# Two softmax attentions with the layers between them issued as jobs by 512 tokens, and inverse roots by Newton steps

## What is computed

```python
h = layernorm(x) * (1 + ca) + sa
y = softmax(mask(rope(h@Wq.T+bq) @ rope(h@Wk.T+bk).T / sqrt(16))) @ (h@Wv.T+bv)   # 16 heads of 16, causal
x = x + ga * (y @ Wo.T + bo)
h = layernorm(x) * (1 + cb) + sb
hidden = h                                   # the second ffn has an attention of its own
a = rmsnorm(hidden, ln1_w)
attn = softmax(mask(heads(a@Wq.T) @ heads(a@Wk.T).T / 4)) @ heads(a@Wv.T) @ Wo.T
mod = 0.1 * tanh(attn @ A)
g = rmsnorm(hidden, ln2_w)
x = x + gb * (hidden + (silu(g@W_in.T + mod*(g@A)@B) * (g@W_up.T)) @ W_down.T)
```

## Time and profile before

| | before |
|---|---|
| time, median of 3 runs (lowest, highest) | 732.89 us (732.44, 736.16) |
| the profiled execution: its own time, its span | 735.81 us, 734.0 us |
| PE busy (share of the span) | 655.8 us (89%) |
| PE weight loads | 415.0 us (57%) |
| DVE, ACT, POOL busy | 473.3 (64%), 347.5 (47%), 169.3 (23%) |
| mean granted TensorE clock | 0.957 |

### The profile page before, as it was taken

The page is one execution under the profiler, slowest core; times in us unless marked ns, Lnnn a source line. Parts: engine busy times, 40 slices in busy tenths (PEclk is TensorE's granted clock), DMA queues, the critical chain, the costliest instruction groups (busy, mean ns, idle before and its releaser), DMA issues.

```text
span 734.0 us, 10645 instructions
## 1 busy us (share of the span) xinstructions
PE 655.8 (89%) x3934; PEld 415.0 (57%) x3939; DVE 473.3 (64%) x955; ACT 347.5 (47%) x558; POOL 169.3 (23%) x209
## 2 busy tenths in 40 slices
PE   4997867999999897699999998787899999999996
PEld 3785635777677676345544434464454444368885
DVE  6777685777677378398888801586589887232323
ACT  4554233443333434325466685462455667843332
POOL 3434214554555235311000000000000001003221
PEclk9999689999999999899999999999799999989998
DMA  8820000002000003733000000026430000050001
GB/s 297 257 71 19 1 21 1 21 23 79 0 1 0 1 1 114 226 93 88 2 2 1 2 2 0 1 82 218 132 89 2 2 2 2 10 165 1 0 1 57
DMA packets 36327, 38.34 MB, mean 52 GB/s; under 512 B 3954, under 2 KB 35200, under 8 KB 36020
## 3 DMA queue, kind: packets, MB, share of 16 engines
q1 hardware_dynamic: 36276, 37.67, 16.3%
HBM read 30.12 MB, written 7.34 MB: 51 GB/s over the span
## 4 chain that ended last, share of the span: by engine, by line
PE 48%; issue 17%; POOL 13%; DVE 11%; ACT 5%; SPq 2%; DMA 2%; POOLq 0%; ACTq 0%; DVEq 0%
PE psum L782 10%; PE psum L768 8%; PE psum L745 8%; POOL it_lo L1700 8%; PE psum L456 3%; PE psum L457 3%; PE psum L458 2%; POOL wd L1675 2%; PE psum L771 2%; SPq L412 2%; PE psum L496 2%; PE psum L748 2%; PE psum L473 2%; POOL t L1650 2%; PE psum L575 1%
## 5 line engine op out<-in xcount | busy, mean ns | idle before, releaser
L966 ACT ACTIVATE pt<-psum 128x1024 f32<-128x1024 f32 (+1 forms) x192 | 148.2, 811 | 94.5 <-PE psum L771 66.1
L1320 DVE TENSOR_REDUCE mx<-psum 128x1 f32<-128x512 f32 (+3 forms) x216 | 132.4, 665 | 16.3 <-PE psum L745 8.3
L745 PE MATMUL psum<-kr,qr 96*128 96x512 bf16 (+3 forms) x384 | 109.9, 336 | 5.2 <-DVE m L1320 1.8
L768 PE MATMUL psum<-qr,kr 99*128 99x512 bf16 (+3 forms) x384 | 99.1, 331 | 5.2 <-DMA qr<-m3T 3.7
L1700 POOL TENSOR_TENSOR it_lo<-it,it_hi 128x512 fp32r<-128x512 f32 x48 | 66.5, 1385 | 153.4 <-ACT it_hi L1017 153.4
L456 PE MATMUL psum<-h_hi,wf_hi 128*128 128x512 f32 x192 | 76.5, 398 | 7.0 <-DVE wf_lo L1381 4.0
L782 PE MATMUL psum<-pt,vp 128*32 128x512 f32 (+3 forms) x768 | 81.7, 498 | 0.0
L1017 ACT CAST it_hi<-it 128x512 fp32r<-128x512 f32 x48 | 29.8, 622 | 97.3 <-DVE it L1393 97.3
L457 PE MATMUL psum<-h_lo,wf_hi 128*128 128x512 f32 x192 | 75.6, 394 | 0.0
L458 PE MATMUL psum<-h_hi,wf_lo 128*128 128x512 f32 x192 | 75.5, 393 | 0.0
L745 PEld LDWEIGHTS psum<-kr,qr 96*128 96x128 bf16 x384 | 36.6, 99 | 68.3 <-DVE mx L1320 29.4
(11 more groups left out here) (209 smaller groups left out, 1132.0 us busy)
## 6 DMA issues: line engine op xcount, KB each, us to landing
parts_scratch<-parts SPq DMA_DIRECT2D x16, 384.0 KB, 3.5
qr<-parts_scratch SPq DMA_DIRECT2D x48, 128.0 KB, 2.6
kr<-parts_scratch SPq DMA_DIRECT2D x48, 128.0 KB, 2.7
wmod<-in_L_wmod SPq DMA_DIRECT2D x1, 1536.0 KB, 6.1
x<-in_L_attn_x SPq DMA_DIRECT2D x2, 512.0 KB, 4.1
wmod<-in_L_wmod SPq DMA_DIRECT2D x1, 1024.0 KB, 7.8
packed<-in_L_ffn_gate_W_packed SPq DMA_DIRECT2D x1, 1024.0 KB, 9.8
packed<-in_L_ffn_up_W_packed SPq DMA_DIRECT2D x1, 1024.0 KB, 11.8
```

What stands on the lines that cost most here:

```text
L745: m = pe.matmul(b, qr[0:PARTS_ROWS, c, h, (qt - 4 * c) * P:(qt - 4 * c + 1) * P], kr[0:PARTS_ROWS, ch, h, 0:w], start=True, stop=not diag)
L768: m = pe.matmul(bank[4 + 2 * at[0] + j][:, 0:w], kr[0:PARTS_ROWS + 3, kt // 4, h, (kt % 4) * P:(kt % 4 + 1) * P], qr[0:PARTS_ROWS + 3, c, ...
L966: act.activation(pt[:, n % 4, :, 0:w], psum[:, b:b + 2, 0:w], ACT.Exp, scale=0.25).then_inc(S["ex"], 1)
L1320: dve.tensor_reduce(dst, bank[at[0]][:, 0:k * w].rearrange("p (k w) -> p k w", k=k), AX, ALU.max).then_inc(S["p1_mx"], 1)
```

## The change

1. `attention_order()` becomes `attention_orders()` and makes one list for each attention. Besides banks, rowmax, scores, values and outs they hold **jobs** (`JOBS`), which are the bridge cut in pieces for 512 tokens. The bridge of tokens 0 to 511 (with the small product `woa` ahead) stands in the list of attention 0, behind `out 3`, when block 3 has finished these tokens. The bridge of tokens 512 to 1023 stands in the list of attention 1, between its blocks of c = 0. A job with a product takes a bank of the ring of three. Banks of c = 1 come in attention 1 only behind the last job of the chain.
2. Both inverse roots are worked out on DVE from a bit pattern and three Newton steps (`inverse_root`): 12 instructions on 128x4, each waiting for the one before it. ACT keeps its table for exp through both attentions.
3. The 42 idle products go. SP writes and spreads tokens 0 to 511 of the second q and k behind the last `row_max` of attention 0, and tokens 512 to 1023 behind `row_max` 3 of attention 1. A few waits keep `qr` and `kr` from being overwritten early. The weights of the second q, k and v are prepared some steps earlier (17, 19, 21 in place of 20, 24, 28).
4. `rest` becomes one buffer per half (both are views of `xn`), and the third set of parts goes.

```diff
+CHAIN = [("att", 0), ("att", 1), ("proj", 0), ("proj", 1), ("upd", 0), ("upd", 1), ("norm", 0), ("ln", 0), ("ln", 1),
+         ("sq", 0), ("sq", 1), ("diag", 0), ("rms", 0), ("prod", 0), ("hi", 0), ("lo", 0),
+         ("qk", 0), ("mid", 0), ("qk", 1), ("low", 0), ("mid", 1), ("qk", 2), ("low", 1), ("mid", 2), ("qk", 3), ("low", 2),
+         ("mid", 3), ("low", 3)]
+VALUES = [[("v", t) for t in range(4 * h, 4 * h + 4)] for h in range(NH)]
+JOBS = [[("woa", 0)] + CHAIN, VALUES[0] + CHAIN + VALUES[1]]
...
+            t = ready_job()
+            if t is not None:
+                choice.append((t, 2, "job"))
+            if banks < len(BANKS) and not (l and BANKS[banks][2] == 1 and jobs < len(JOBS[l]) - 4):
+                choice.append((ring, 3, "max"))
...
+                if l and half == 0 and dt == 0:
+                    sp.wait_ge(S["p1_s"], BANKS_END[5])
+                    sp.wait_ge(S["s2"], 2 * STEPS_END[5])
...
+                    if l and half == 0 and dt == 1 and is_k:
+                        sp.wait_ge(S["p1_s"], len(BANKS))
+                        sp.wait_ge(S["s2"], 2 * len(STEPS))
...
+                    elif what == "qk":
+                        pe.wait_ge(S["ln_hl"], 12 + 2 * half + 2)
+                        pe.wait_ge(S["wt_lo"], 10)
+                        c0 = i % 2 * D + i // 2 * P
+                        tok = slice(half * HALF, (half + 1) * HALF)
+                        for kc in range(KC):
+                            m = mm3(b[:, :], w_hi[:, kc, c0:c0 + P], w_lo[:, kc, c0:c0 + P],
+                                    h_hi[:, kc, tok], h_lo[:, kc, tok], kc == 0, kc == KC - 1)
+                        m.then_inc(S["qt"], 1)
...
-            idle(18, 4)
-            layer_norm(3, 0)
-            layer_norm(3, 1)
...
+            def inverse_root(src, scale, eps, dst, n):
...
+                dve.tensor_scalar(v, src, scale, eps, ALU.mult, ALU.add).then_inc(S["nw"], 1)
...
+                for j in range(3):
+                    old, new = y0 if j == 0 else y, dst if j == 2 else y
+                    dve.wait_ge(S["nw"], at + 3 * j + 3)
+                    dve.tensor_tensor(a, old, v, ALU.mult).then_inc(S["nw"], 1)
+                    dve.wait_ge(S["nw"], at + 3 * j + 4)
+                    dve.scalar_tensor_tensor(b, a, -0.5, old, ALU.mult, ALU.mult).then_inc(S["nw"], 1)
+                    dve.wait_ge(S["nw"], at + 3 * j + 5)
+                    dve.scalar_tensor_tensor(new, b, 1.5, old, ALU.add, ALU.mult).then_inc(S["nw"], 1)
+                dve.wait_ge(S["nw"], at + 12)
...
+                elif what == "diag":
+                    dve.wait_ge(S["ss_ok"], 4 * half + 4)
+                    inverse_root(ss[:, tiles], 1.0 / D, 1e-6, rs[:, tiles], 2 * half + 1)
```

More of the change, by code:

```diff
@@ L84, in attention_order, with attention_orders @@
+COST = {"att": (440, 590, 0), "proj": (1710, 750, 0), "upd": (440, 0, 1600), "norm": (0, 0, 5000), "ln": (440, 750, 0),
+        "sq": (440, 800, 0), "diag": (0, 0, 3800), "rms": (870, 600, 0), "prod": (0, 0, 1400), "hi": (0, 1200, 0),
+        "lo": (0, 0, 1400), "qk": (1370, 590, 690), "mid": (0, 600, 0), "low": (0, 0, 690), "v": (720, 380, 0),
+        "woa": (400, 350, 0)}
+def attention_orders():
     hop = 200.0
-    order, used = [], 0
+    orders, used = [], 0
     holder, freed = [None] * RING, [0.0] * RING
@@ L119, in ready_value @@
[L119 to L164, removed]
-            i, half = divmod(scores, 2)
[L166 to L185, removed]
@@ L192, in build @@
+    return orders
+ORDERS = attention_orders()
 def build(nc, a, out):
@@ L264, in build @@
         wf_lo = [wf_lo2[:, 0, :], wf_lo2[:, 1, :], wf_lo1[:, :]]
-        part_sets = [[[z[:, n, :, :] for n in range(4)] for z in (parts, other)] for other in (parts2, parts3)]
+        part_sets = [[[z[:, n, :, :] for n in range(4)] for z in (parts, other)] for other in (parts2, parts)]
         t1 = sb("t1", [P, 2, HALF])
@@ L733, in attention @@
                 loaded = []
-                for what, i, *at in ORDER:
+                for what, i, *at in ORDERS[l]:
                     if what == "max":
@@ L842, in _ @@
-            pe.wait_ge(S["rb_ok"], 2)
-            for t in range(NT):
-                if t >= 2:
-                    pe.wait_ge(S["vp_e"], 8 + t - 1)
-                token_major(t, bank[5 + 2 * (t % 2)][:, 0:D], 512, 768).then_inc(S["vj"], 1)
+                    elif at and what not in ("copy",):
+                        bank_free(at[1])
+                        chain(l, what, i, bank[at[0]])
+                if l == 1:
+                    pe.wait_ge(S["p1_mx"], len(BANKS) * 2)
+            attention(0)
@@ L935, in split @@
                     if n < 4:
-                        act.wait_ge(S["qt"], 8 * l + 4 * half + n + 1)
-                        if l == 1 and half == 0 and n == 0:
-                            for dt in range(2):
-                                act.wait_ge(S[f"pw{dt}"], 16 * 4)
-                        act.copy(part_sets[l][half][n][:, (0, 1)[n % 2], :], bank[n][:, :]
+                        act.wait_ge(S["qt"], 4 * half + n + 1)
+                        act.copy(part_sets[0][half][n][:, (0, 1)[n % 2], :], bank[n][:, :]
                                  ).then_inc(S["sp_h"], 1)
@@ L951, in attention @@
             def attention(l):
-                act.activation(sd[:, 0:1], minus1[:, :], ACT.Exp)
-                for what, i, *at in ORDER:
+                if l == 0:
+                    act.activation(junk[:, 3:4], minus1[:, :], ACT.Exp)
+                for what, i, *at in ORDERS[l]:
                     if what == "score":
@@ L984, in attention @@
                         act.copy(osb[:, n % 2, :], bank[3][:, :]).then_inc(S["ob"], 1)
+                    elif what not in ("max", "value", "out"):
+                        chain(l, what, i, bank[at[0]] if at else None)
             def mlp_weights_hi(f, i):
@@ L1341, in attention @@
                             rd[:, :, :].unsqueeze(3).to_broadcast([P, 4, 4, DH]), ALU.mult).then_inc(S["att_w"], 1)
+                    elif what not in ("score", "value", "rowmax", "copy"):
+                        chain(l, what, i, bank[at[0]] if at else None)
             def dequantise_bits(i):
```

518 lines of the change are left out of this document (342 added, 176 removed).

## The result

The changed kernel takes 756.5 us (median of 4 runs, 755.7 to 760.1), the kernel before 734.5 on the same chip: a ratio of 1.031 (95% interval 1.027 to 1.035), 22 us slower. The forecast was 741.8, 8.9 us over the 732.89 that it started from. The side was right, the size was not. The profiled execution took 760.06 us against 735.81.

What follows compares the result with a forecast made beforehand. PE was taken to set the pace, DVE close behind. Removing the bridge (-53.1), attention 0 (+20.5) and attention 1 (+41.5) gave +8.9 us on the median of 732.89, so 741.8 us; range 724 to 757.

Steps and rivals of the forecast that it cites:

- Rival 1: Whole kernel: PE has room, so jobs go into its gaps; 719.6 us, chance 0.25.
- PE term of 15.5: Attention 0: PE time in us of the bridge steps put there, summed from their products and transposes.
- (b): Attention 1: first bank of c = 1 waits for the reads with PE otherwise idle; 11 us, bounds 10 and 14.
- (c): Attention 1: 32 banks to the next rowmax at DVE's pace; 24 us taken, bounds 20 and 28.
- (a): From attention 0's last out to the end of `low 3` in attention 1; 65 us, bounds 55 and 74.
- Rival 2: Turns come out even: (a) at 60 and `diag` hidden in attention 0; 733 us, chance 0.15.
- rival 4: Change fails its aim, e.g. attention 1's reads come late and the stall comes twice; 753 us, chance nearly nothing.
- a gap at `diag`: Attention 0: block 5's scores wait behind the root step on DVE; 5 to 6 us of PE lost, 5 taken.
- upper bound of 27: Attention 0's largest forecast growth in us, from 12 waits of DVE for ACT; the forecast was +20.5.
- (d): Last piece of attention 1, order as before; 84.7 us, bounds 83 and 88.
- At nothing: Costs counted as zero: SP's waits, two table loads of 1.28 us beside other work, and the idle products.
- Rival 3: DVE jams: each `qk`, `mid` and `low` makes DVE and ACT wait for each other; 759 us, chance 0.12.

Runs made afterwards that it cites:

- a0_late: Changed kernel with some chain steps held back in attention 0 and reads of heads 0 to 7 issued earlier for tokens 0 to 511: 745.1 us, ratio 1.015.
- spin_all: Changed kernel with idle products at three PE waits and one ahead of each of 27 banks of block 4 in attention 1: 753.8 us, ratio 1.025.

## Why the prediction was right in its side and wrong in its size

**Right.** The direction, by its reason: the bridge held little lost time, and the new places of its steps lose more. Rival 1 (PE has room) fell: in `a0_late`, where hardly anything waits, the steps put into attention 0 cost 16.2 us for 15.7 us more of PE time (96.9 against 81.2), so PE's time is paid in full. The share of weight loads is 44% there, and the rule of the Trainium skill, *Perfetto Trace Analysis*, *Identifying the Most-Contended Engine*, read so that this share alone leaves room, does not hold in this stretch. (The page names the rate of useful work, MFU, beside it, which was not worked out here.) The PE term of 15.5 was right. Piece (b) came to 10.8 (11 forecast), (c) to 25.2 (24), (a) to 68.6 (65), all within their bounds. Rival 2 fell with attention 0 and (a), and rival 4 did not occur: behind the last out of attention 0 PE waited for no read until the first bank of c = 1.

**Wrong: attention 0 beyond PE's own work, where the sum had only "a gap at `diag`", "I take 5".** Attention 0 cost 29.1, not 20.5, and lies over the upper bound of 27. Over PE's own 15.7 it lost 13.4: 7.9 more idle time of PE and 5.5 in work that ran slower. The gap itself was sized rightly: in the 16.0 us without an exp PE was idle for 5.3. The step that failed is that the sum ended there. The waits of PE at other steps (the other 2.6) and what a wait does to the work behind it (5.5) stood at nothing. 2.8 us of the latter are the granted clock, which was 0.67 and 0.65 in and behind the gap and 0.50 once more over 463 to 466, ahead of the last out; `spin_all` gives their price. `a0_late` shows that the loss is one of place: the same instructions, with the roots and the split where DVE's maxima run out, lose 0.5.

**Wrong by less: attention 1,** 190.8 against 184.7. 3.6 of it are in (a), 1.5 in (d), 1.2 in (c). In (a) PE waits 4.4 us for the norm, at `rowmax 0`; the clock fell there too, and keeping it up at this place and at the reads gave 4.2 us back. (c) was right for its reason: DVE is full there, with 20 banks and then 11 in a row:

```profile
569.94 11.62 DVE L1497 TENSOR_REDUCE mx<-psum 128x1 f32<-128x512 f32 x20
581.59 0.19 DVE L1501 TENSOR_REDUCE m<-mx 128x16 f32<-128x32 f32 x1
581.70 6.86 DVE L1497 TENSOR_REDUCE mx<-psum 128x1 f32<-128x512 f32 x11
```

**"At nothing" for the table loads** was right: in the kernel before they hid nothing. The Newton steps, which the sum had only in DVE's queue at `diag` (2.5), cost the kernel before 6.0 us in place of ACT's roots. What they cost the changed kernel in place of ACT's was not tried; three more steps in each root cost it some 4.1 us.

**Rival 3** named the time (759) and half the cause. DVE does not jam at each `qk`, `mid` and `low`; it holds PE at the two long steps, `diag` and `norm`. And the stall that I counted as given, 10.8, can be filled: with scores and values held back for it, and later places for steps in attention 0, the change is worth 0.8 to 1.0% instead of costing 3.1.

## What to carry to other kernels

When a serial stretch is cut into jobs among an attention's products, count first what overlapped in it: here two halves took 53 us and one alone 50 (41 to 50 by the estimate above), so hiding one half saves little until the other is hidden too. Then place the jobs by the engine that they hold up: long steps of VectorE belong where its own queue runs dry, and work that depends on nothing (scores held back) where the DMA round trip leaves PE alone. An order's planner that has no price for the DMA round trip spends that work too early.

## What was not expected of the hardware

The granted clock was 1.00 from 327 to 401, and behind a stretch in which PE was busy 0.66 of 4.4 us its work ran at 0.65. In the order without idle products eight transposes of 128 x 128 took 1.97 us behind 4.05 us of waiting, against 1.25 with 3.40 us of idle products ahead. So single waits of 3.5 to 4 us were followed by slower work here. What this costs is small and differs from run to run: 2.8 us in attention 0, of which 1.6 were there in some runs and not in others with the same instructions, and 4.2 at two places of attention 1. Idle products are slowed by the clock as well: 14 of them took 3.19 us in one run and 4.88 in another, 20 took 4.49 and 6.18, and when they outlast the wait that they cover, what they were to give back is gone. Placed 3 us behind the wait that they were meant for, 20 products of 4.6 us cost 5.2.
